# Perceiver layer: another order of stage 1 on all engines, a gate product in fp32r parts, a third context buffer

## What is computed

```
x = x + xattn(layernorm(x), ctx)        # ctx: 128 x 257 x 256
x = x + scan(layernorm(x))
x = x + ffn(layernorm(x))

xattn: Sim = hc.w1 + hq.w2 + (hc*w3) hq^T + b;  A = softmax(Sim);  hq_hat = A hq
       hc_bar = softmax(max Sim) pooled hc       # one vector per sequence
       out = [hc, hq_hat, hc*hq_hat, hc*hc_bar] W_qv + b_qv
scan:  xg = x * sigmoid(x Wg^T + bg);  s_t = s_(t-1) A + xg_t Bp;  y = s_t.Cp + Dp*xg_t
       out = layernorm(y + xg) * gamma + beta
ffn:   h = bitlinear(x, w_fc) + gate * low rank;  out = bitlinear(relu(h)^2, w_proj)
```

## Time and profile before

| | |
|---|---|
| median of 3 runs | 538.97 us (538.63 to 540.72) |
| profiled execution: its own time | 538.89 us |
| its span | 536.4 us |
| PE busy | 479.4 us (89%) |
| DVE busy | 419.9 us (78%) |
| ACT busy | 359.4 us (67%) |
| POOL busy | 343.9 us (64%) |
| TensorE clock granted, mean | 0.98 of full |
| moved by DMA | 70.38 MB, mean 131 GB/s |

### The profile page before, as it was taken

The page is one execution under the profiler, slowest core; times in us unless marked ns, Lnnn a source line. Parts: engine busy times, 40 slices in busy tenths (PEclk is TensorE's granted clock), DMA queues, the critical chain, the costliest instruction groups (busy, mean ns, idle before and its releaser), DMA issues. The chain is left out here.

```text
span 536.4 us, 13420 instructions
## 1 busy us (share of the span) xinstructions
PE 479.4 (89%) x4310; PEld 402.2 (75%) x4310; DVE 419.9 (78%) x1159; ACT 359.4 (67%) x854; POOL 343.9 (64%) x444
## 2 busy tenths in 40 slices
PE   2397799999999999999999996876799999999996
PEld 2275687888887877687787875765588888888885
DVE  1398888888888999999998884457677987988654
ACT  2555578676876767677676766555578768768753
POOL 1377767676775757756756664503578878888653
PEclk9789999999999999999999999998899999999999
DMA  6734445756584555555645568259502022011102
GB/s 206 197 114 149 138 151 160 219 156 217 145 234 136 177 169 139 191 146 139 199 136 144 194 200 178 60 133 218 125 1 79 1 80 79 26 55 39 41 1 78
DMA packets 81316, 70.38 MB, mean 131 GB/s; under 512 B 39760, under 2 KB 64608, under 8 KB 81248
## 3 DMA queue, kind: packets, MB, share of 16 engines
q1 hardware_dynamic: 81248, 69.54, 45.4%
HBM read 56.87 MB, written 12.65 MB: 130 GB/s over the span
## 5 line engine op out<-in xcount | busy, mean ns | idle before, releaser
L1647 POOL TENSOR_TENSOR sq_lo<-scan_x,sq_hi 128x512 fp32r<-128x512 f32 x63 | 82.7, 1313 | 33.6 <-ACT sq_hi L1619 33.6
L705 PE MATMUL turn_ps<-ident,ctxn 128*128 128x128 f32 x512 | 70.3, 282 | 4.4 <-DMA ctxn<-in_ctx 4.4
L933 ACT COPY ctxT<-turn_ps 128x512 f32<-128x512 f32 x128 | 68.2, 583 | 5.4 <-PE turn_ps L705 5.4
L705 PEld LDWEIGHTS turn_ps<-ident,ctxn 128*128 128x128 f32 x512 | 58.2, 144 | 18.0 <-issue 13.2
L1611 ACT ACTIVATE relu<-fc_ps,fc_square 128x512 f32<-128x512 f32 x64 | 43.8, 684 | 31.0 <-PE fc_ps L1545 30.9
L1689 DVE SCALAR_TENSOR_TENSOR scan_x<-fc_ps,relu 128x512 f32<-128x512 f32 x64 | 43.8, 684 | 26.0 <-ACT relu L1611 25.5
L1121 POOL TENSOR_TENSOR hc_lo<-hc_probT,hc_hi 128x256 fp32r<-128x256 f32 x32 | 23.4, 731 | 61.0 <-ACT hc_hi L942 60.9
L1541 PE MATMUL fc_ps<-xn_hi,fc_T 128*128 128x512 f32 x128 | 52.1, 407 | 2.1 <-DVE scan_x L1689 2.1
L1107 POOL TENSOR_TENSOR rstd<-ve,neg_half 128x1 f32<-128x1 f32 x64 | 35.2, 550 | 27.6 <-DVE ve L1331 17.7
L1541 PE MATMUL fc_ps<-xn_lo,fc_T 128*128 128x512 f32 x128 | 51.1, 399 | 0.0
L1113 POOL TENSOR_TENSOR proj_in<-proj_in,below 128x512 f32<-128x512 f32 x31 | 49.3, 1592 | 0.0
(11 more groups left out here) (227 smaller groups left out, 1400.8 us busy)
## 6 DMA issues: line engine op xcount, KB each, us to landing
ctxn<-in_ctx SPq DMA_DIRECT2D x32, 1024.0 KB, 5.5
resid<-in_x SPq DMA_DIRECT2D x32, 128.0 KB, 5.2
ctx_end<-in_ctx SPq DMA_DIRECT2D x32, 128.0 KB
gated_tokens<-gated SPq DMA_DIRECT2D x32, 128.0 KB, 6.2
scan_x<-gated_tokens SPq DMA_DIRECT2D x60, 64.0 KB, 4.9
out<-resid SPq DMA_DIRECT2D x7, 512.0 KB, 3.1
scan_tokens<-scan_x SPq DMA_DIRECT2D x12, 256.0 KB, 5.1
y_in<-scan_tokens SPq DMA_DIRECT2D x4, 512.0 KB, 4.8
```

What stands on the lines that cost most here:

```text
L705: mm = pe.transpose(turn_ps[b % 2][:, (c * JT + t) * P:(c * JT + t + 1) * P], ctxn[p][:, b, t, c * P:(c + 1) * P], ident[:, :])
L933: act.copy(ctxT[:, b, :, 0:J - 1], turn_ps[b % 2][:, :].rearrange("p (k j) -> p k j", k=KD)).then_inc(ctxT_copied, 1)
L1647: pool.tensor_tensor(sq_lo[:, m, :], sq[m % SQ], sq_hi[:, m, :].bitcast(F32), ALU.subtract).then_inc(sq_lo_done, 1)
```

## The change

Stage 1 is put in another order on every engine. On PE the scores come right behind attention, behind all four context transposes; the products of `hc` move ahead, and the rest of a group is `z`, `hq` transposed, the products of `hb`, the gate, `hq`, `hcq`. `hc` and `prob` are transposed and copied apart. The gate's product is made of six fp32r products of high and low parts. Its low parts `zT_lo` and `wgT_lo` are made by DVE. The context has three buffers; the third is lent by the first 16 channels of `toeplitz`, which is therefore zeroed later, in eight parts: six in groups 4 to 9, two in group 31. Each of groups 1 to 29 takes one state step, groups 8 and 11 two. `state_sum` stands behind `layer_norm1`, POOL's `state_product` ahead of both powers, `weights(g)` between `dot1` and `neg_max`, and the impulse response behind `normalise1` in group 30. At the end SP stores the second half of piece 0 behind the last scan load, and DVE normalises x's first chunk before it sums y's second. The rest of the diff joins semaphores, turns unused loop forms into plain ones and lets small tiles share memory (`z`, `hcqT`, `bg_all`).

```diff
+            DEEP = 3
+            LENT = NB * JT * D // P
+            ctxn = [sb(f"ctxn{p}", [P, NB, JT, D], scope=s1) for p in range(DEEP - 1)]
+            ctxn.append(toeplitz[:, 0:LENT, :].rearrange("p (b t k) j -> p b t (k j)", b=NB, t=JT))
+            TWICE = (8, 11)
+            STATE_FIRST = 1
+            ZERO_PARTS = 8
+            ZERO_FIRST = 4
 SP
-                    if inside or g + 2 < GROUPS:
+                    if g + DEEP < GROUPS:
                         at_least(sp, attended, g + 1)
-                        load_ctx(g + 2, p)
+                        load_ctx(g + DEEP)
...
                 store_piece(sp, 0, 0, PB // 2, first_stored[0])
-                store_piece(sp, 0, PB // 2, PB // 2, first_stored[1])
                 step(GROUPS + 1, 0, ())
...
                 scan_load(sp, GROUPS - 1, 1)
+                store_piece(sp, 0, PB // 2, PB // 2, first_stored[1])
                 sp.wait_ge(first_stored[1], 16 * NB)
 PE
+                def sum_gate(g):
+                    pe.wait_ge(zT_hi_ready, g + 1)
+                    pe.wait_ge(zT_lo_ready, g + 1)
+                    for i, (part, w) in enumerate(((zT_hi, wgT_hi), (zT_hi, wgT_lo), (zT_lo, wgT_hi))):
+                        for c in range(KD):
+                            mm = pe.matmul(gate_ps[:, 0:D], part[:, c, :], w[:, c, :], start=(i == 0 and c == 0),
+                                           stop=(i == 2 and c == KD - 1))
+                    mm.then_inc(gate_summed, 1)
+                def step(g):
...
+                        turn_context(g, 0)
+                        turn_context(g, 1)
+                    if has_b:
+                        turn_prob(g)
+                        pool_hc(g)
+                    if has_b and g > 1:
+                        project_hc(g)
+                    if has_a:
+                        turn_context(g, 2)
+                        turn_context(g, 3)
+                    if has_b:
+                        attend(g)
+                    if has_a:
+                        score(g)
+                    if has_c:
+                        turn_z(g - 2)
+                    if has_b:
...
+                        project((hb_hi, hb_lo), 3)
+                    if has_c:
+                        sum_gate(g - 2)
+                    if has_b:
+                        project((hq_hi, hq_lo), 1)
+                        project((hcq_hi, hcq_lo), 2, last=True).then_inc(projected, 1)
 ACT, step: hc copied; ctxT 0, 1; prob copied; hcwT; ctxT 2, 3; then
+                    if has_b:
+                        act.copy(hb_hi[:, :, :], hbT[:, :, :]).then_inc(hb_hi_ready, 1)
+                    if has_c:
+                        make_z(g - 2)
+                        copy_zT(g - 2)
+                    if has_b:
...
...
+                    if has_c:
+                        tanh_gate(g - 2)
+                    if has_a:
+                        act.copy(hc_hi[:, :, :], hc_probT[p][:, 0, :, :]).then_inc(hc_hi_ready, 1)
 ACT, end
-                for n in range(6, 8):
-                    y_block(n)
+                y_block(6)
                 tanh_gate(GROUPS - 1)
 POOL, step: hc_lo; state_product; rstd2; rstd1; end column; hb_lo; beta; b_qv; second state_product; hcq_lo; then
+                    if ZERO_FIRST <= g < ZERO_FIRST + ZERO_PARTS - LENT_PARTS:
+                        zero(g - ZERO_FIRST + LENT_PARTS)
+                    if g == GROUPS - 1:
+                        pool.wait_ge(attended, GROUPS - 2)
+                        for part in range(LENT_PARTS):
+                            zero(part)
 DVE, step: x1, bn2, mv2, ve2; layer_norm1(g + 1); then
+                    for s in state_steps[:1]:
+                        state_sum(s)
...
+                    if g + 1 < GROUPS:
+                        normalise1(g + 1)
+                    if g == GROUPS - 2:
+                        impulse_response()
...
+                    if g + 1 < GROUPS:
+                        dot1(g + 1)
+                    weights(g)
...
+                    if has_c:
+                        at_least(dve, zT_hi_ready, g - 1)
+                        at_least(dve, gate_summed, g - 2)
+                        dve.tensor_tensor(zT_lo[:, :, :], gate_ps[:, 256:256 + D].rearrange("p (k t) -> p k t", k=KD),
+                                          zT_hi[:, :, :].bitcast(F32), ALU.subtract).then_inc(zT_lo_ready, 1)
+                    if g == 1:
...
+                    if has_b:
+                        at_least(dve, hq_hi_ready, g)
+                        low_rank_in(g)
...
+                    for s in state_steps[1:]:
+                        state_sum(s)
...
 DVE, end
                 x_moments(dve, 0)
+                norm_first(dve)
                 y_sums(dve, 1, range(CH))
                 y_moments(dve, 1)
-                norm_first(dve)
```

More of the change, by code:

```diff
@@ new lines, in project_hc, with turn_prob @@
+                def project_hc(g):
+                    at_least(pe, hc_hi_ready, g)
+                    at_least(pe, hc_lo_ready, g)
+                    at_least(pe, x1_ready, g - 1)
+                    project((hc_hi, hc_lo), 0, first=True).then_inc(hc_projected, 1)
+                def turn_prob(g):
+                    at_least(pe, prob_ready, g)
+                    at_least(pe, hc_copied, min_groups(g + 1))
+                    for t in range(JT):
+                        mm = pe.transpose(side_ps[:, 256 + t * P:256 + (t + 1) * P],
+                                          prob[(g - 1) % 2][:, t * P:(t + 1) * P], ident[:, :])
+                    mm.then_inc(prob_turned, 1)
@@ new lines, in pool_hc @@
+                def pool_hc(g):
+                    at_least(pe, pick_ready, g)
+                    at_least(pe, hq_hi_ready, g - 1)
+                    at_least(pe, hq_lo_ready, g - 1)
+                    if g == LOW_GROUP:
+                        pe.wait_ge(w_loaded, 16 * W_LOADS)
+                        for c in range(KD):
+                            low = pe.matmul(low_ps[:, c * RANK:(c + 1) * RANK], v_in[:, c * P:(c + 1) * P], fbT[:, :],
+                                            start=True, stop=True)
+                        low.then_inc(low_product, 1)
+                    for c in range(KD):
+                        mm = pe.matmul(feat_ps[:, 256 + c * NB:256 + (c + 1) * NB], hc[(g - 1) % 2][:, c * P:(c + 1) * P],
+                                       pick[:, :], start=True, stop=True)
+                    mm.then_inc(pooled, 1)
@@ new lines, in attend @@
+                def attend(g):
+                    at_least(pe, prob_copied, g)
+                    at_least(pe, hq_ready, g - 1)
+                    at_least(pe, dot_done, min_groups(g + 1))
+                    for t in range(JT):
+                        for b in range(NB):
+                            mm = pe.matmul(att_ps[b * L:(b + 1) * L, 0:D], hc_probT[g % 2][:, 1, t, b * L:(b + 1) * L],
+                                           ctxn[(g - 1) % DEEP][:, b, t, :], start=(t == 0), stop=(t == JT - 1))
+                    mm.then_inc(attended, 1)
@@ new lines, in score @@
+                def score(g):
+                    at_least(pe, ctxT_copied, g * 4 + 4)
+                    at_least(pe, end_placed, g + 1)
+                    at_least(pe, hcwT_ready, g + 1)
+                    at_least(pe, neg_max_ready, g)
+                    at_least(pe, exp_done, g)
+                    for c in range(KD):
+                        for b in range(NB):
+                            mm = pe.matmul(score_ps[b * L:(b + 1) * L, 0:J], hcwT[:, c, b * L:(b + 1) * L],
+                                           ctxT[:, b, c, :], start=(c == 0), stop=(c == KD - 1))
+                    mm.then_inc(scored, 1)
@@ L899, in _ @@
                 for g in range(GROUPS + 1):
[L900 removed]
+                    step(g)
                 for n in range(4):
```

521 lines of the change are left out of this document (224 added, 297 removed).

## The result

The changed kernel took 543.18 us (median of nine runs, 541.36 to 544.34), the kernel before 539.34 beside it (nine runs, 538.10 to 542.48): ratio 1.006, 95% interval 1.003 to 1.009. It is slower, by a little over the 0.5% that can be told from no change. The forecast was 535.0, the range 525 to 541.5: the time lies outside it, on the other side of no change. The profiled execution took 543.29 us, and its span is 541.4, against 536.4 before: 5.0 more.

What follows compares the result with a forecast made beforehand. Context transfers were no bound: PE ran gapless in ordinary groups, `prob` was held early, DVE was full in ternary groups. Terms +0.7 - 8.2 + 1.1 + 0.6 + 2.3 - 2.8 + 2.5 = -3.8 gave 535 us, range 525 to 541.5.

Steps and rivals of the forecast that it cites:

- PE's time and the gate's wait: Ordinary group: PE alone 8.62 us, but the gate stalls 0.46 for `zT_lo`; period 9.08, a change of -0.05.
- rival A: Ordinary and ternary groups: `zT_lo` in time, ternary pair between POOL's instructions, PE sets the pace; 521.5 us, chance 0.2.
- Groups 2 to 4, 5 to 13, 14 to 18: Stage 1: early groups become ordinary, -8.2 us; double state products cost +1.1; earlier sums of magnitudes cost +0.6.
- Rivals B and C: B: POOL's state product delays `rstd`, 546.5 us, chance 0.12. C: early groups don't shrink, 541 us, chance 0.08.
- Group 1: First group: more work ahead of attention, and `wgT_lo` ahead of `hq_lo` on DVE; +0.7 us (0 to 2).
- Ternary groups: Groups 19 to 26: ternary pair now ahead of `neg_max`, 10.2 us each, held end 10.4; +2.3 us (-3.4 to +4).
- Group 27 to the first scan block: End of stage 1's groups: 30 longer, 31 ordinary, step 32's attention free of window placing; -2.8 us (-4.5 to 0).
- The end: Scan block to stage 3: SP's four moved stores and their landing wait (about 1.5 us) make SP last; +2.5 us.
- rival D: End of stage 1: SP's queue doesn't close it and DVE's earlier finish counts; 531 us, chance 0.2.
- Stage 3 at nothing: Stage 3 (165 us) keeps its code, so its time was forecast not to change.
- The third buffer at nothing: Context loading in stage 1: no wait for the context left to remove, so the third buffer costs nothing.
- Rival E: Attention joined to scores: issue pace binds, 32 matmuls take 2.0 us instead of 1.72; 543 us, chance 0.03.

Runs made afterwards that it cites:

- the second combination: Changed kernel, three buffers kept, with old SP order, gate in plain fp32, weight work behind `hcqT`, impulse response at end of group 30: 524.07 us, 0.972 of before.
- experiments 3 and 4: experiment 3, then two tries in the changed kernel: `z` earlier on ACT and PE with `zT_lo` ahead of `hcqT`, 551.46 us; only that DVE swap, 550.66 us.
- experiment 2: Kernel before, with only POOL's zeroings (eight of half size, groups 4 to 11) and state steps (one per group, two in 8 and 11) moved: 536.09 us.
- experiment 3: Changed kernel with the gate in plain fp32, `zT_lo` and `wgT_lo` no longer made: 537.68 us.
- experiment 6: Changed kernel with two context buffers, all eight zeroings in groups 4 to 11: 568.19 us; with attention also ahead of the last two context transposes: 562.83 us.
- experiment 7: Changed kernel with the impulse response moved back behind the gated tile of group 30: 540.99 us.
- experiment 5: Changed kernel with DVE's weight work (magnitude sums, scales, ternary pair) moved back behind `hcqT` and `zT_lo`: 534.10 us, 0.990 of before.
- experiment 1: Changed kernel with SP's old order at the end, second half of piece 0 stored right behind the first: 538.91 us, 0.999 of before.
- the three combinations: Changed kernel with several steps undone together: one with two buffers, 556.61 us; the second combination, 524.07 us; the latter with two late orders changed further, 523.12 us.

## Why the prediction was wrong, by its steps

**PE's time and the gate's wait: right.** 9.08 was forecast and 9.11 is the period, with a gap before the gate put down to `zT_lo`. Joining shows: attention starts 0.89 before the scores, and the scores 0.98 before `z`, 1.87 for both, near the forecast 1.9, and 0.14 less than apart (1.00 and 1.01 in the earlier trace rows), at the low end of the prediction's 0.14 to 0.20. PE without that wait needs 8.98 with the gate in fp32; by the prediction's figures it would be 8.62 + 0.14 = 8.76. The 0.14 was too small: with no change of tiles ahead of them the four fp32 passes still take 0.97 (309.38 to 310.35 in the second combination), so six fp32r products save 0.25, not 0.14. What the prediction lacked is that `hcqT`, `hq_hi` and `hq_lo` form one chain with the gate's wait (experiments 3 and 4), so that the order of DVE tried there could not bring rival A.

**Groups 2 to 4, 5 to 13, 14 to 18: right**, -8.1, +1.4, +0.3, and experiment 2 shows the first by itself. Rivals B and C fell: in DVE's waits `rstd` holds `hc` twice, 1.4 us in all, and groups 2 to 4 take 9.11 each.

**Group 1: mis-sized**, +1.9 for +0.7. `wgT_lo` makes `hq_lo` late, and PE waits 1.18 us for it; without `wgT_lo` 0.7 to 1.2 comes back (experiment 3, by the run it is set against).

**Ternary groups: right in kind, 1.2 short.** The forecast gave 10.4 as the held end, took 10.2, and 10.36 came, with operations of 0.82 and 0.85. The step that failed is the choice of a value inside the bounds although POOL's three operations back to back had been read off.

**Group 27 to the first scan block: failed**, +0.1 for -2.8, the largest error. Groups 27 to 30 are 0.5 longer than forecast, the rest lies in "31 is then ordinary, 9.1, and attention of step 32 no longer waits behind the placing of windows: 9.3": 20.76 came for 18.4. Timeline of PE in the kernel before, then those of the changed kernel (DVE and POOL, then ACT, then PE):

```profile
330.97 1.07 PE L767 MATMUL att_ps<-ctxn,hc_probT 128*32 128x256 f32 x16 [2.10 <-ACT hc_probT L950]
333.81 0.69 PE L778 MATMUL gate_ps<-ident,z 128*128 128x128 f32 x2 [1.77 <-ACT z L969]
```

```profile
326.57 1.51 DVE L1458 TENSOR_SCALAR prob<-prob,row_rec 128x257 f32<-128x257 f32 x1
```
```profile
326.09 1.84 POOL L1150 MEMSET toeplitz<- 128x1024 f32 x2
```
```profile
330.52 2.11 ACT L954 COPY toeplitz<-ctxn 32x1024 f32<-32x1024 f32 x2 [1.54 <-DMA ctxn<-impulse]
```
```profile
333.62 0.44 PE L793 MATMUL gate_ps<-ident,xn 128*128 128x128 f32 x2 [2.19 <-ACT xn L965]
...
336.21 0.63 PE L801 MATMUL gate_ps<-wgT_hi,zT_lo 128*128 128x256 f32 x2
336.63 0.63 PE L729 MATMUL qv_ps<-proj_T,hq_hi 128*128 128x256 f32 x2
```

Group 31 is not ordinary: the two zeroings of the lent part hold `prob` for 1.5 us, the mechanism of the earlier trace rows, which the prediction did not look for here. But by experiment 6 this costs next to nothing: without it PE waits longer for `z`. What sets the stretch is the landing of the windows. ACT waits for them until 12.37 us after the start of group 31, places two rows (2.11), casts `hb_hi` and only then makes `z`. In the kernel before they had landed after 11.62 us, although the impulse response was stored 3.8 us later: the loads wait for attention (experiment 7), which now stands later in the step. Before, PE waited for this twice, 2.10 ahead of attention and 1.77 ahead of `z`; now attention runs free and `z` waits 2.19. All of PE's waits from group 31 to the scan block are 5.0 us before and 3.5 after: part of the stall went, and what is left stands at the next in ACT's queue, which the prediction did not name.

The other part is the clock. After this wait PE's products start 0.43 us apart, not 0.24: this is the lower of TensorE's two levels, 1.2 for 2.4 GHz. The kernel before had it too (granted clock 0.50 from 334 to 337), but the forecast doesn't speak of it. From the gate's first product to the scan block it is 3.69 us here and 2.36 in experiment 5, where the clock was not lowered: 1.3 of the missing 2.4. The 1.8 by which the stretch is shorter in experiment 5 is this and a `z` that comes 0.5 sooner (a wait of 1.70), with windows that landed 0.5 sooner. Windows of the profile, of the changed kernel and of experiment 5's (window and length, busy time of PE, PEld, DVE, ACT, POOL, granted clock, DMA share, GB/s):

```profile
334.00:339.00 5.00, 4.80 (x31) 4.49 (x33) 2.03 (x5) 2.70 (x6) 4.52 (x5) 0.66 0.44 94
```
```profile
325.00:329.00 4.00, 3.79 (x32) 3.48 (x32) 2.03 (x5) 2.00 (x5) 3.79 (x5) 1.00 0.47 95
```

**The end: failed**, +4.7 for +2.5. Place and direction were right (SP is last), and rival D fell; the last scan load is issued 3.6 us sooner after the first scan block (3.5 forecast). The mis-sized term is "the wait for their landing (about 1.5)": from the end of issue to the landing it is 4.1 us, and the page of the changed kernel gives such a store a median of 4.6 from issue to landing:

```profile
scan_tokens<-ctxn SPq DMA_DIRECT2D x8, 128.0 KB, 4.6
```

The Trainium skill (DMA: Bandwidth & Descriptors, "Anatomy of one DMA") gives a fixed cost of about 2 us, for transfers issued by GpSimd, and would have been short here too; the measurement decides.

**Stage 3 at nothing: failed by 1.1.** Its code is the same, its start is not. Next rows of PE in stage 3, in the kernel before and in the changed one:

```profile
374.83 0.77 PE L1533 MATMUL xt_ps<-xn_hi,low_in 128*128 128x512 f32 x1 [2.58 <-DVE xn_lo L1673]
```
```profile
379.79 0.61 PE L1586 MATMUL xt_ps<-xn_hi,low_in 128*128 128x512 f32 x1 [2.73 <-DVE xn_lo L1726]
```

The first eight transposes take 1.06 us before and 1.94 after (the earlier trace rows and the rows above), and the next product starts 3.64 and 4.68 us into the stage: 1.0 of the 1.1. The granted clock in the first four microseconds is 0.97 before and 0.50 after. PE had waited 1.05 us for the other engines before and 9.28 after. All runs agree: in the nine in which these transposes take 1.94 us, behind a wait of 3.6 to 10.8 us, stage 3 takes 166.3 to 166.7; in the other five (the kernel before, experiment 2 and the three combinations) they take 1.06 to 1.29, behind 0.7 to 1.5 us, and stage 3 takes 164.9 to 165.8. The prediction said that "DVE and PE would be 1 to 2 us early, and wait" and gave that wait no price.

**The third buffer at nothing** was right as a term and wrong as a reading: "no wait for the context is left to remove" held for the old place of attention. In the new one the buffer is worth 25 us.

**Rival E** fell: the joined 32 matmuls take 1.87, not 2.0.

## What to carry to other kernels

When an edit lets one instruction pass a late event, read who else stands behind that event on the same queue, and read what the event itself waits for: producing its input sooner gains nothing if it waits for something else too. When stores are moved behind a later event and something waits for their landing, price the landing from a row of issue to landing, not by feel. A long wait of TensorE can have a second price, the products behind it at the lower clock. An operation's place also sets its length where two engines share memory: put it where the other one is idle.

## What the runs showed that was not expected

- The ternary pair takes 1.67 us beside POOL and 0.83 where POOL is idle for most of it, on the same data: moving it 1.4 us later in the group gave 6.7 us in eight groups.
- Two 128x128 transposes between the halves of the scores cost 0.23 more than behind them (1.48 for 1.25). As an estimate that is two more changes between tile shapes, 0.12 each, a little below the 0.14 to 0.20 taken from the earlier trace rows.
- In step 32 PE's wait for `z` was followed by a lower clock in the changed kernel (2.19 us) and in experiment 1 (1.74 us, mean granted clock 0.66 from 333 to 338), and by none in experiment 5 (1.70 us) and in the second combination (2.05 us). The length of this one wait doesn't decide it; what does stays open.
